# Background work beside attention, issued greedily or at a pace

## What is computed

```
x0 = x0 + g_msa0 * mha(mod(ln(x0)))          # 1024 rows, the same for x1
x  = x + (g_mca0 * attend(qx, ky, vy) @ w, g_mca1 * attend(qy, kx, vx) @ w)
x  = x + g_mlp * (gelu(mod(ln(x)) @ fc1 + b) @ fc2 + b)
x  = ln(x + mha(x, x, x, mask))              # second block
x  = ln(x + mha(x, ctx, ctx))                # 1601 keys
x  = ln(x + relu(x @ w1 + b1) @ w2 + b2)
```

## Time and profile before

| | us |
|---|---|
| median of 3 runs | 2312.32 |
| profiled execution | 2312.77 |
| its span, first to last instruction | 2310.9 |
| TensorE busy | 2056.0 |
| VectorE busy | 1565.6 |
| ScalarE busy | 1286.7 |
| end of the last attention unit | 2231.7 |

### The profile page before, as it was taken

One profiled execution on the slowest core, in us unless ns is written; L12 is line 12 of the kernel. 1 busy time (PEld: TensorE's weight loads), 2 busy tenths in 40 slices (PEclk: granted clock), 3 DMA queues, 4 the chain that ended last, 5 costly groups with the idle time before them and its releaser, 6 DMA issues. The chain is left out here.

```text
span 2310.9 us, 33848 instructions
## 1 busy us (share of the span) xinstructions
PE 2056.0 (89%) x12890; PEld 801.7 (35%) x12890; DVE 1565.6 (68%) x2867; ACT 1286.7 (56%) x2406; POOL 472.1 (20%) x464
## 2 busy tenths in 40 slices
PE   4788999899889999989998898999899999999975
PEld 2423233322133353533523442332253334334324
DVE  3477999787666848467465556886757995896703
ACT  1035776565445677645774562578335884684650
POOL 0024333333132201023112331220203101101100
PEclk8669999998799999999999996999789999999987
DMA  7615323412034202035014531200202010000000
GB/s 158 120 62 113 91 62 99 103 61 75 16 90 100 70 3 55 8 70 131 3 46 94 100 97 36 56 20 5 49 5 54 18 33 18 13 16 4 13 15 11
DMA packets 97305, 126.66 MB, mean 55 GB/s; under 512 B 25293, under 2 KB 81982, under 8 KB 92014
## 3 DMA queue, kind: packets, MB, share of 16 engines
q1 hardware_dynamic: 97134, 124.42, 22.7%
HBM read 89.95 MB, written 24.74 MB: 50 GB/s over the span
## 5 line engine op out<-in xcount | busy, mean ns | idle before, releaser
L1576 ACT ACTIVATE PT<-ps 128x512 f32<-128x512 f32 (+1 forms) x2112 | 1099.4, 603 | 734.8 <-PE ps L1361 728.5
L1645 DVE TENSOR_REDUCE mx<-ps 128x1 f32<-128x512 f32 x2048 | 1281.3, 682 | 290.4 <-PE ps L1382 287.0
L1382 PE MATMUL ps<-KS,QS 49*128 49x512 bf16 x2048 | 550.0, 408 | 134.1 <-DVE mx L1645 92.1
L1361 PE MATMUL ps<-QS,KS 51*128 51x512 bf16 (+3 forms) x4224 | 621.7, 391 | 21.1 <-DMA QS<-mr 20.7
L1408 PE MATMUL ps<-PT,Vt 128*32 128x512 f32 (+1 forms) x4224 | 587.0, 628 | 0.0
L1382 PEld LDWEIGHTS ps<-KS,QS 49*128 49x128 bf16 x2048 | 148.7, 95 | 739.6 <-DVE mx L1645 517.3
L1361 PEld LDWEIGHTS ps<-QS,KS 51*128 51x128 bf16 (+3 forms) x4224 | 210.5, 97 | 285.3 <-ACT PT L1576 82.6
L1885 POOL CAST nm<-nm 128x16 bf16<-128x16 f32 x64 | 12.6, 196 | 668.1 <-DVE nm L1658 668.1
L1408 PEld LDWEIGHTS ps<-PT,Vt 128*32 128x32 f32 (+1 forms) x4224 | 84.8, 109 | 151.9 <-issue 148.5
L1503 PE MATMUL ps<-XT,big 128*128 128x256 f32 x512 | 129.0, 404 | 2.3 <-ACT big L1618 1.4
L1467 PE MATMUL ps<-XT,wA 128*128 128x512 f32 (+1 forms) x216 | 109.5, 634 | 8.7 <-DMA wA<-in_L_xattn_sa_qw 6.2
(11 more groups left out here) (106 smaller groups left out, 1126.4 us busy)
## 6 DMA issues: line engine op xcount, KB each, us to landing
scr<-S SPq DMA_DIRECT2D x28, 768.0 KB, 3.6
big<-in_mask_1x1xSxS_ik SPq DMA_DIRECT2D x16, 1024.0 KB, 4.9
QS<-scr SPq DMA_DIRECT2D x32, 384.0 KB, 8.8
KS<-scr SPq DMA_DIRECT2D x24, 384.0 KB, 8.6
QS<-scr SPq DMA_DIRECT2D x32, 256.0 KB, 4.9
ON<-Oe SPq DMA_DIRECT2D x256, 32.0 KB
OD<-scr_r SPq DMA_DIRECT2D x32, 256.0 KB
KS<-scr SPq DMA_DIRECT2D x24, 256.0 KB, 4.9
```

Of the source, the lines that this page charges most:

```text
L1361: z = eng.matmul(ps[0:w, it.bank[j], :], KS[lo:hi, part, pr, col:col + w], QS[lo:hi, part, u.qs, pr, :], start=part == 0, stop=part == 1 a ...
L1382: return eng.matmul(mbank(it)[:, 0:w], QS[lo:lo + MR, 0, u.qs, pr, 128 * it.tq:128 * it.tq + 128], KS[lo:lo + MR, 0, pr, it.lo:it.hi], sta ...
L1576: eng.activation(PT[0:w, it.pt * 4 + 2 * it.pp + j, :], ps[0:w, it.bank[j], :], ACT.Exp, scale=0.25).then_inc(S["exp_done"], 1)
L1645: eng.tensor_reduce(out=mx[:, u.b, c, it.i:it.i + 1], in_=mbank(it)[:, 0:it.hi - it.lo], axis=AX.X, op=ALU.max).then_inc(S["max_done"], 1)
```

## The change

1. Each piece has a third entry, its weight (1 for two halves of matmuls, 0 for norms, loads and markers). `Track.pace` adds to a credit in each step, and a piece with a weight goes out only while the credit is above 0, and then takes its weight from it. A forced piece pays nothing. `ends_track` has its credit set to 1 in every step.
2. The output projection of a chunk is two pieces in different steps, no longer two items in one.
3. `do_mout` is two pieces of 16 matmuls, one row tile each, instead of one of 32. The residual behind it has one tile too.
4. The hidden pieces of an MLP all wait 1 step. Before, the third went in the same step as the second.
5. The last MLPs of chunks 2 and 3 are due at units 57 and 62, not 99.

```
+PACE = 0.12
+SPARE = 12
+            def pace(self, step, begin_of):
+                todo = Counter({self.due: sum(e[2] for e in self.cur)})
+                for due, _, chain, _ in self.queue:
+                    todo[due] += sum(e[2] for e in chain)
+                need, total = PACE, 0.0
+                for due in sorted(todo):
+                    total += todo[due]
+                    need = max(need, total / max(1, begin_of(due) - step - SPARE))
+                self.credit = min(1.0, self.credit + need)
...
-                    elif (norms if wait is None else wait > self.since):
+                    elif (norms if wait is None else wait > self.since) or (self.cur[0][2] and self.credit <= 0):
                         return
-                    self.cur.pop(0)[1]()
+                    _, piece, weight = self.cur.pop(0)
+                    piece()
+                    if not force:
+                        self.credit -= weight
...
-        def bg_step():
+        def bg_step(step, begin_of):
...
+            work.pace(step, begin_of)
+            ends_track.credit = 1.0
             ends_track.step()
             work.step()
...
-                    bg_step()
+                    bg_step(step, lambda unit: opens[max(0, unit - unit0[0])] if unit - unit0[0] < total else step_total)
...
-            return [(1, lambda: half(0)), (1, second)]
+            return [(1, lambda: half(0), cols / 512), (1, second, cols / 512)]
...
-            return [(1, lambda t0=t0: tiles(t0)) for t0 in range(0, nt, 2)]
+            return [(1, lambda t0=t0: tiles(t0), min(1, (nt - t0) / 2)) for t0 in range(0, nt, 2)]
...
+            return [(None, lambda: two(0), 1), (1, lambda: two(2), 1)]
...
-            return [(d, f) for hf in range(2) for d, f in
-                    [(2 - hf, lambda hf=hf: do_hid(c, relu, bc, hf, 0))]
-                    + [(hp % 2, lambda hf=hf, hp=hp: do_hid(c, relu, bc, hf, hp)) for hp in range(1, 4)]
-                    + [(2, lambda hf=hf: do_mout(c, hf, gate, gbi))]]
+            was = {}
+            return [e for hf in range(2) for e in
+                    [(1, lambda hf=hf, hp=hp: do_hid(c, relu, bc, hf, hp), 1) for hp in range(4)]
+                    + [(2 - t, lambda hf=hf, t=t: do_mout(c, hf, t, gate, gbi, was), 1.75) for t in range(2)]]
...
-            return [(1, lambda: do_stats(c, 1e-6)), (3, lambda: do_xnorm(c)), (3, lambda: do_xt("mod", c, g))]
+            return [(1, lambda: do_stats(c, 1e-6), 0), (3, lambda: do_xnorm(c), 0), (3, lambda: do_xt("mod", c, g), 0.6)]
...
-            return ([(0, load), (0, lambda: need_kv("ca")), (8, lambda: do_xt("ctx", 4, 0, cols))]
+            return ([(0, load, 0), (0, lambda: need_kv("ca"), 0), (8, lambda: do_xt("ctx", 4, 0, cols), 0.6 * cols / 512)]
...
-                work.post(99, [(f"ca{c}", lambda: None)] + mlp1(c))
+                work.post({2: 57, 3: 62, 0: 99, 1: 99}[c], [(f"ca{c}", lambda: None, 0)] + mlp1(c))
...
-                    for t in range(2):
-                        for hc in range(8):
-                            z = eng.matmul(mbank(it)[:, 256 * t:256 * t + 256], HT[:, hc, 128 * t:128 * t + 128],
-                                           w2[:, hc, :], start=hc == 0, stop=hc == 7)
+                    for hc in range(8):
+                        z = eng.matmul(mbank(it)[:, 0:256], HT[:, hc, 128 * it.t:128 * it.t + 128], w2[:, hc, :],
+                                       start=hc == 0, stop=hc == 7)
```

More of the change, by code:

```diff
@@ L512, in residual, with out_steps, two @@
             mark["gb_free", gbi[0]] = (f"x_done{c}", it.done)
[L514 to L518, removed]
+        def out_steps(c, gate, gbi):
+            was = {}
+            def two(lo):
+                flush_slow()
+                if lo == 0:
+                    was["x"], was["xn"] = n[f"x_done{c}"], mark["xn_free"]
+                else:
+                    at["out"] = 0
                 it = item("out")
@@ L522, in do_out @@
                 mark["od_free"] = mark["wp_free"] = it.m_ready
-                residual(it, c, lo, 2, gate, gbi, x_done, xn_free)
+                residual(it, c, lo, 2, gate, gbi, was["x"], was["xn"])
+            return [(None, lambda: two(0), 1), (1, lambda: two(2), 1)]
         def do_lnscale(c, gl, b):
@@ L547, in do_hid, with do_mout @@
             give_m(it, (name, up(name)))
-        def do_mout(c, hf, gate, gbi):
+        def do_mout(c, hf, t, gate, gbi, was):
             flush_slow()
+            if t == 0:
+                was["x"], was["xn"] = n[f"x_done{c}"], mark["xn_free"]
             it = item("mout")
+            it.t = t
             it.act, it.dve, it.w = n["ht_act"], n["ht_dve"], n["w2_in"]
@@ L554, in do_mout @@
             mark["ht_free"] = mark["mlp_free"] = it.m_ready
-            residual(it, c, 2 * hf, 2, gate, gbi, n[f"x_done{c}"], mark["xn_free"])
+            residual(it, c, 2 * hf + t, 1, gate, gbi, was["x"], was["xn"])
         def mlp_chain(c, relu, bc, gate, gbi):
-            return [(d, f) for hf in range(2) for d, f in
-                    [(2 - hf, lambda hf=hf: do_hid(c, relu, bc, hf, 0))]
-                    + [(hp % 2, lambda hf=hf, hp=hp: do_hid(c, relu, bc, hf, hp)) for hp in range(1, 4)]
-                    + [(2, lambda hf=hf: do_mout(c, hf, gate, gbi))]]
+            was = {}
+            return [e for hf in range(2) for e in
+                    [(1, lambda hf=hf, hp=hp: do_hid(c, relu, bc, hf, hp), 1) for hp in range(4)]
+                    + [(2 - t, lambda hf=hf, t=t: do_mout(c, hf, t, gate, gbi, was), 1.75) for t in range(2)]]
         def load_wA(parts, vbias):
@@ L636, in __init__ @@
                 self.queue, self.cur, self.since, self.due, self.key = [], [], 0, 0, None
+                self.credit = 0.0
+            def pace(self, step, begin_of):
[7 more added lines that the diff above has]
+                self.credit = min(1.0, self.credit + need)
             def post(self, due, chain, rank=1, key=None):
@@ L738, in drain @@
             flush_norms()
-            for _, f in chain:
-                f()
+            for e in chain:
+                e[1]()
             flush_later()
@@ L764, in attention @@
             opens = [0] + [max(begin[k - 1] + 1, begin[k - 1] + size[k - 1] - LEAD) for k in range(1, total)]
+            step_total = sum(size)
             k, left, m, step, held = 0, [], 0, 0, None
@@ L825, in x_q @@
         def x_q(c, slot, p):
-            return [(0, lambda: need_q(p)), (3, lambda: do_xt("x", c))] + q_steps(c, slot, 8 if p == "sa" else 12)
+            return [(0, lambda: need_q(p), 0), (3, lambda: do_xt("x", c), 0.6)] + q_steps(c, slot, 8 if p == "sa" else 12)
         def out_l0(c, g):
             norm(c % 2)
-            ch = [(None, lambda: do_out(c, g, (g % 2, c // 2)))]
+            ch = out_steps(c, g, (g % 2, c // 2))
             if g == 1:
-                ch = [(0, lambda: reload_x(c))] + ch
+                ch = [(0, lambda: reload_x(c), 0)] + ch
             return ch
@@ L975, in xattn_kernel @@
         work.post(8, q_l0(2, 0, 0), 2)
-        work.post(8, q_l0(3, 1, 0) + [(0, lambda: l0_weights("crs"))], 3)
+        work.post(8, q_l0(3, 1, 0) + [(0, lambda: l0_weights("crs"), 0)], 3)
         side.extend([lambda t=t, k=k: scan(t, k) for t in range(NT) for k in range(4)])
@@ L999, in crs_start @@
                 load_mlp(I["L0_xattn_mlp_fc1_w"], I["L0_xattn_mlp_fc2_w"])
-            work.post(17, out_l0(3, 0) + [(0, lambda: slow.append([6, crs_start]))])
+            work.post(17, out_l0(3, 0) + [(0, lambda: slow.append([6, crs_start]), 0)])
             work.post(20, kv_l0(3, 1, 1))
@@ L1016, in row @@
                     mark["k", "row_in"] = ("row_in", it.landed)
-                return ([(0, weights), (4, lambda: do_xt("x", 3))] + k_steps(0, 512, "k_insa", over, 8)
-                        + v_steps(0, 512, "sa", over) + [(4, row)])
+                return ([(0, weights, 0), (4, lambda: do_xt("x", 3), 0.6)] + k_steps(0, 512, "k_insa", over, 8)
+                        + v_steps(0, 512, "sa", over) + [(4, row, 0)])
             def l1_out_start():
@@ L1031, in post @@
                 if c == 2:
-                    work.post(25, out_l0(2, 1) + [(0, lambda: slow.append([6, lambda: gate_bias(2, I["L0_xattn_mlp_fc2_b"])]))])
+                    work.post(25, out_l0(2, 1) + [(0, lambda: slow.append([6, lambda: gate_bias(2, I["L0_xattn_mlp_fc2_b"])]), 0)])
                     work.post(28, mlp0(2))
@@ L1046, in post @@
                 else:
-                    work.post(36, out_l0(1, 1) + [(0, lambda: slow.append([6, l1_out_start]))], 0)
+                    work.post(36, out_l0(1, 1) + [(0, lambda: slow.append([6, l1_out_start]), 0)], 0)
                     work.post(44, ctx_kv(1, 512, 4, now()))
                     work.post(44, ctx_kv(2, 512, 4, now()))
-                    work.post(44, [("sa2", lambda: None)] + x_q(2, 1, "ca"), 0)
+                    work.post(44, [("sa2", lambda: None, 0)] + x_q(2, 1, "ca"), 0)
```

(4 more changed lines are left out.)

6 lines of the change are left out of this document (3 added, 3 removed).

## The result

The changed kernel takes 2403.2 us (median of 4 runs, 2397.1 to 2407.4) against 2312.4 (2306.0 to 2315.0) for the kernel before: a ratio of 1.039, interval 1.037 to 1.042. The forecast was 2350, with a range that ended at 2385. The sign was right and the size was not: +91 us where +37 was expected.

What follows compares the result with a forecast made beforehand. TensorE was taken as the bound, with VectorE also at its limit in quiet 8-tile units, so work only moves: 2312.8 - 14 - 4 - 12 - 3 + 6 + 3 + 61 = 2349.8, said as 2350 us (+1.6%), range 2270 to 2385.

Steps and rivals of the forecast that it cites:

- Forced points: Query or key rows late for units 20, 48, 44, 32 and 16, so TensorE waits: 61 us slower, 15 to 90.
- Tables: Gelu and exp table loads on ScalarE, 8 more groups at 0.77 us of TensorE idle: 6 us, 0 to 45.
- rival B: Each of 32 lone gelu groups stops exponentials for 3.4 us and TensorE for 1.4: 2389 us, chance 0.09.
- Split pieces: Two products of 16 matmuls cost what one of 32 did; residuals' added fixed costs find room: nothing.
- Bubbles that go: Norm statistics behind the output projection: two of five TensorE bubbles go, 14 us, the other three shrink, 4 us.
- Smoother mixing: Spread pieces fill TensorE's idle time in quiet 8-tile and ca units: 12 us gained, 16 at most.
- The last units: Chunk 0's relu MLP runs on into unit 63, 2 us free; shorter tail, about 1: together 3 us gained.
- Cold units: Unit at 1653.86: chunk 2's relu MLP parts, paced over units 51 to 55, are paid in full: 3 us more, 0 to 6.

Runs made afterwards that it cites:

- The right aim: The change's pace aimed at opens of the unit before, where bg_until forces, with all pieces of before: 2315.3 us, against 2364.7 with the changed kernel's aim.
- the greedy kernel: The kernel before, unpaced, with one edit: each third hidden piece of an MLP half chunk in a step of its own; 2331.9 us (1.010).
- pairs of gelu pieces: The kernel before with the four gelu hidden pieces of a half chunk in two groups instead of three: 2297.8 us, measured again at 2295.6 (0.993).
- pairs of relu pieces: The kernel before with hidden pieces in pairs in the relu chunks too, beside the gelu pairs: 2309.9 us (1.000).

## Why the prediction was wrong, point by point

- **Forced points: +61 forecast, and they held as a mechanism.** TensorE waited for `QS<-scr` in units 18 and 46 and for `KS<-scr` at unit 44's keys, at the places named: 17.3, 17.5 and 13.7 us where 16, 18.6 and 9.6 had been worked out without the clock. The two small ones came out at 6.5 (unit 32, for 5) and 9.6 (unit 16, for 4.4 + 5). The idle time of the five is 60 us more than before. The right aim was worth 49 us (a wait of 5.1 us at unit 44 stays with it), so the term was 12 too high, within its bounds. It had left out that waits elsewhere shrink when these grow: with the pieces of before and the changed pace the five waits are 65.8 us more than before and TensorE's idle time as a whole only 54.4 more (309.3 for 254.9).
- **Tables: +6 forecast, and this is the term that failed.** They cost the changed kernel 2403.2 - 2363.1 = 40 us and the kernel before 8.3, so the change brought 32. The forecast took the price of a group from one place, where TensorE's idle time beside it was 0.77 us. It multiplied this by the 8 groups added. For the 24 groups that were there the price was no underestimate (8.3 us, 0.35 each), but it doesn't hold for the ones added, which cost 3.0 us each in the greedy kernel. The right question was how full ScalarE is in that stretch: each group added puts 2.57 us of loads into a stretch in which the two engines are level. The upper end, 45 us for 32 groups, had the right mechanism and was given to rival B with a chance of 0.09. B's 2389 is nearest to the measured time because it adds dear tables to the late rows, and both were there. "It has 5 us to spare in each unit" fits the quiet unit of the earlier trace rows (22.37 - 16.90) and not the gelu unit (56.32 - 40.63), and inside the MLP's own steps there is nothing to spare.
- **Split pieces: nothing forecast, +18 measured** (7.9 for the MLP's product, 10.4 for the output projection). The matmuls did cost what they had (388 ns a matmul at L1543, for 382). Two loads were waited for longer, `wA` for 11.4 us (6.2 before) and `QS<-mr` for 25.8 in all (20.7 before). That they come later because a chain of more steps ends later is likely, but no run shows it by itself.
- **Bubbles that go: -18 forecast, hardly anything gained.** VectorE's wait for the last sum did shrink, from 11.5 us in 5 to 4.0 in 3, as forecast:
```profile
DVE st L1697 <- POOL x L1959: 4.0, 3, 1.4
```
  But TensorE still stands five times, for 3.15, 2.75, 3.72, 2.81 and 3.03 us, 15.5 us for 18.2. In the two places where another chunk's chain now comes between, VectorE waits a few us later instead, at the normalisation, for GpSimd's split of that chain's rows, since the norm writes to the buffer `xn` that the split still reads:
```profile
855.19 1.38 DVE L1708 TENSOR_SCALAR xn<-x,mv,rs 128x256 f32<-128x256 f32 x4 [2.52 <-POOL S L1941]
857.23 0.61 PE L1412 MATMUL ps<-KS,QS 49*128 49x512 bf16 x1 [3.72 <-DVE mx L1674]
```
  The forecast took these two bubbles as gone in full, at 6.9 us each, and didn't ask what VectorE would wait for next.
- **Smoother mixing: -12 forecast, nothing found.** The pace with the right aim and all old pieces measured +4.5, with an interval that just reaches 0.
- **The last units: -3 forecast.** Unit 63 does hold an MLP product now, 16 matmuls of 3.72 us in all, at 30.80 us for 27.46, so only 0.4 us of it was free, where 2 were forecast. The tail is 78.5 us for 79.3, as forecast.
- **Cold units: +3 forecast.** No run takes this term by itself. The unit at 1750.11, the same as that of 1653.86 before, takes 41.71 us for 43.04, at a clock of 0.54 for 0.52.

By the runs the sum is 49 for late rows, 32 for tables, 18 for split pieces: 99 against 91 measured, and the 8 us between are within what these differences are uncertain by. By its own steps the forecast is 26 too low for tables, 18 for split pieces, about 15 for bubbles and 12 for mixing, and 12 too high for the rows: 59, where 53 were missing.

What stays open: how the 18 us of the split pieces divide between later weights, later rows and clock, what a bubble is worth if it goes without a delay elsewhere, what pairs of gelu pieces save beside table loads, and why pairs of relu pieces lose 12 us.

## What to carry to other kernels

Price an added piece of work on a second engine by that engine's busy share inside the very steps where it goes, not by the idle time that one existing piece shows, nor by its mean over a longer unit. Here it was nearly free up to the level at which both engines are full, and cost its full time beyond. Before pacing background work, check that the point a pace aims at is the point at which it is forced, less the full latency of the last result: here one unit's difference in the aim was worth 49 us, and the pace as such nothing. And before counting a bubble in the timeline as a gain, ask what the engine behind it will wait for next, and whether the work that is moved is wanted early elsewhere.

## What the runs showed of the hardware

- A load of the exponential's table starts within 0.02 us of the end of the gelu before it (1121.80 and 1121.82 above), also when ScalarE is full (17.98 of 18.30 us), so a change to gelu and back costs two loads of 1.28 us and nothing between. The Trainium skill (ScalarE: Activation LUTs, "What ACT_TABLE_LOAD costs") adds a drain of 1.38 us a switch. No trace here has it. By that page 16 more switches would be an estimated 43 us of ScalarE. In the greedy kernel they cost 24 us. The Trainium skill's advice in "Rules for kernel authors" on the same page, to do all work of one table set before switching, agrees in its direction with two groups for three (-15.4 us) and with one for three (2301.7, -9.8 us), though one group is not better than two and the gain is more than the loads were worth.
- The price of table loads is far from proportional to their number. 48 loads are worth 8 us, 64 loads 32 us in a greedy kernel and 40 in a paced one.
